# Narrow-head attention on Trainium2: the value products of a step in two bursts of two heads instead of one burst of four

## The chip, the cores and the metric

The kernel runs on one core of one Trainium2 chip. The metric is the device time of one execution in microseconds; the median of several runs is given. The engines are TensorE (matmuls and weight loads), VectorE, ScalarE, GpSimd and the DMA queues, each with an instruction stream of its own, and they meet at semaphores.

## What is computed

The program is a stack of four pre-norm transformer layers on an input of 4 x 1024 tokens with 128 features. Only the attentions of the first two layers are touched. Both have 16 heads of 8 features; layer 0 is causal, layer 1 is not:

```python
scores = jnp.einsum('bthd,bshd->bhts', q, k) / math.sqrt(dk)
scores = jnp.where(causal_mask, jnp.float32(-jnp.inf), scores)   # layer 0
attn = jax.nn.softmax(scores, axis=-1)
out = jnp.einsum('bhts,bshd->bthd', attn, v).reshape(Bx, Tx, D)
...
scores = jnp.einsum('bhqd,bhkd->bhqk', q, k) * SCALE             # layer 1
scores = scores - jnp.max(scores, axis=-1, keepdims=True)
attn = jnp.exp(scores)
attn = attn / jnp.maximum(jnp.sum(attn, axis=-1, keepdims=True), 1e-12)
ctx = jnp.einsum('bhqk,bhkd->bhqd', attn, v)
```

## The kernel before

`narrow_attention` is called for layer 0 (causal) and for layer 1. Its work is cut into 16 units, one for each batch and each group of four heads. A unit needs two things of every query: first the maximum of its scores, then the exponentials and their products with the values.

**The maxima, a unit ahead.** `a_slot` (L1181) multiplies a block of 128 queries with up to 512 keys into one of three banks `slot_ps`, and VectorE reduces it to `part_max` (L1344; L1340 with the mask on the diagonal of layer 0). A unit has 64 such slots in layer 1 and 48 in layer 0. They are worked off four to a step during the steps of the unit before (`shape.ahead`), `lead` = 5 or 6 steps early. Behind the last slot `max_turn` (L1188) transposes the maxima, GpSimd splits them into three bf16 parts, and DMAs put them into `q_op` as extra rows, so that the score product subtracts them.

**The steps.** A step is half the queries (512, `hq`) against one block of 128 keys (`kb`), for all four heads: 16 steps a unit in layer 1; 12 in layer 0, where future blocks are left out and the four blocks on the diagonal of each half stream only 512, 384, 256 and 128 queries. Score products (L1203) are bf16 with 51 rows, two heads `jj` in the two row halves of the array; the pair `e` = 0 or 1 of heads goes to the bank pair `scores[e]`. On the diagonal of layer 0 four small mask products (L1210, 128 columns) follow each pair. ScalarE takes the exponential of a pair (L1321) into `probs`, in one of four buffers, and counts `probs_done`.

**The values.** `values(u, n)` (L1223) multiplies the values of a block with `probs`, in float32, 32 columns of the array for each head, so that the four heads lie in four column groups and write four stripes of one bank `o_ps`. It accumulates over the blocks of a half. At the first block of a half it waits until ScalarE has copied the former half out of the bank (`o_copied`, L1308). Every float32 product is two records in the trace, so a call leaves eight. When a half is done, `o_turn` (L1195) transposes the copy and VectorE divides by the sums.

**The order on TensorE in step n of unit u** is written out by hand. For e = 0: one slot, the score pair 0 (after waiting for the exponential of pair 0 of the step before), one slot. For e = 1 the same. Then the values of step n - 1, all four heads. Then, at three of the steps, a turn. ScalarE's order is: at the second step of a half the copy of the former half, then the two exponentials.

Of the kernel before, what the change touches and what calls it, by code (L numbers as in the profile page):

```python
# [27 lines left out]
UNITS = BATCH * GROUPS  # L28
# [1052 lines left out]
def narrow_attention(nc, name, shape, operands, scale, ctx_nat, consts, floor=None, fills=None, soft=None):  # L1081

    H, S, BANKS = 4, shape.n, 3
    NA = len(shape.slots)
    feats = ctx_nat.shape[1] // TILES
    with ExitStack() as ctx:
# [6 lines left out]
        def sem(n):  # L1093
            return nc.alloc_semaphore(f"{name}_{n}")
# [23 lines left out]
        scores_ready, probs_done, pv_done = sem("scores_ready"), sem("probs_done"), sem("pv_done")  # L1118
# [47 lines left out]
        @block.tensor  # L1166
        def _(te):
            def bank_for(n):
                if n >= BANKS:
                    te.wait_ge(slot_done, n - BANKS + 1)  # L1170
                return slot_ps[n % BANKS]

            def a_slot(u, s):

                j, qt, kh = shape.slots[s]
                g, e, r0 = u % GROUPS, j // 2, (j % 2) * HALF_ROWS
                if s == 0:
                    te.wait_ge(qk_loaded[g], (u // GROUPS + 1) * 16 * N_QK)
                out = bank_for(shape.place["slot", u, s])
                width = shape.slot_width(s)  # L1180
                nc.tensor.matmul(out[:, 0:width], q_op[g][r0:r0 + MAX_ROW, e, qt * P:(qt + 1) * P],  # L1181
                                 k_op[g][r0:r0 + MAX_ROW, e, kh * CH:kh * CH + width], start=True, stop=True).then_inc(slot_ready, 1)

            def max_turn(u):

                te.wait_ge(row_max_done, u + 1)
                out = bank_for(shape.place["max", u, 0])
                nc.tensor.transpose(out[0:H * KB, 0:P], row_max[:], ident[:]).then_inc(slot_ready, 1)  # L1188

            def o_turn(u, hq):  # L1190

                te.wait_ge(o_copied, u * 2 + hq + 1)
                out = bank_for(shape.place["o", u, hq])
                for t in range(CPT):
                    mm = nc.tensor.transpose(out[:, t * P:(t + 1) * P], o_sb[hq][:, t * P:(t + 1) * P], ident[:])  # L1195
                mm.then_inc(slot_ready, 1)

            def score(u, n, e, jj):

                hq, kb = shape.steps[n]  # L1200
                g, off, r0, r1 = u % GROUPS, shape.off(hq, kb), jj * HALF_ROWS, jj * HALF_ROWS + MAX_ROW + 3
                diag = shape.causal and kb >= CPT * hq
                return nc.tensor.matmul(scores[e][:, jj, off:CH], k_op[g][r0:r1, e, kb * P:(kb + 1) * P],  # L1203
                                        q_op[g][r0:r1, e, hq * CH + off:(hq + 1) * CH], start=True, stop=not diag)

            def mask(n, e, jj, h):

                hq, kb = shape.steps[n]
                off, r0 = shape.off(hq, kb), jj * HALF_ROWS
                return nc.tensor.matmul(scores[e][:, jj, off:off + P], ident2[r0:r0 + HALF_ROWS, h, :],  # L1210
                                        mask_b2[r0:r0 + HALF_ROWS, h, :], start=False, stop=h == 1)

            def values(u, n):

                hq, kb = shape.steps[n]
                g, off = u % GROUPS, shape.off(hq, kb)
                te.wait_ge(probs_done, (u * S + n + 1) * 2)
                if n == 0:
                    te.wait_ge(v_spread, u + 1)
                if kb == 0 and u * 2 + hq > 0:  # L1220
                    te.wait_ge(o_copied, u * 2 + hq)
                for j in range(H):
                    mm = nc.tensor.matmul(o_ps[32 * j:32 * (j + 1), off:CH], v_op[g][:, kb, 32 * j:32 * (j + 1)],  # L1223
                                          probs[(u * S + n) % NB][:, j, off:CH], start=kb == 0, stop=n in shape.half_end)
                mm.then_inc(pv_done, 1)

            if shape.causal:
                te.wait_ge(masks_loaded, 48)
            for s in range(NA):
                a_slot(0, s)  # L1230
            max_turn(0)
            for s in shape.head_start():
                a_slot(1, s)
            te.wait_ge(ones_loaded, 16 * 2 * R)
            for u in range(UNITS):
                te.wait_ge(max_loaded[u % GROUPS], (u // GROUPS + 1) * 16 * N_MAX)
                for n in range(S):
                    todo = shape.ahead(u, n)
                    cut = [len(todo) * p // 4 for p in range(5)]
                    gs = u * S + n  # L1240
                    hq, kb = shape.steps[n]
                    diag = shape.causal and kb >= CPT * hq
                    for e in range(2):
                        for v, s in todo[cut[2 * e]:cut[2 * e + 1]]:
                            a_slot(v, s)
                        if gs > 0:
                            te.wait_ge(probs_done, (gs - 1) * 2 + e + 1)
                        score(u, n, e, 1)
                        mm = score(u, n, e, 0)
                        if diag:  # L1250
                            mask(n, e, 1, 0)
                            mask(n, e, 0, 0)
                            mask(n, e, 1, 1)
                            mm = mask(n, e, 0, 1)
                        mm.then_inc(scores_ready, 1)
                        for v, s in todo[cut[2 * e + 1]:cut[2 * e + 2]]:
                            a_slot(v, s)
                    if n > 0:
                        values(u, n - 1)
                    elif u > 0:  # L1260
                        values(u - 1, S - 1)
                    if n == 2 and u > 0:
                        o_turn(u - 1, 1)
                    if n == shape.half_end[0] + 3:
                        o_turn(u, 0)
                    if n == S - shape.lead and u + 1 < UNITS:
                        max_turn(u + 1)
            values(UNITS - 1, S - 1)
            o_turn(UNITS - 1, 1)

        @block.gpsimd
# [688 lines left out]
class CosineShape:  # L1960


    S = 2 * KB
# [1272 lines left out]
```

## Time and profile before

| | |
|---|---|
| median of 3 runs | 3596.66 us (3596.16 to 3596.76) |
| the profiled execution | 3575.11 us, its span 3573.2 us |
| busy in the span | PE 83%, DVE 73%, ACT 60%, POOL 13% |
| attention of layer 0, first to last exponential | about 107.8 to 553 us |
| attention of layer 1, first to last exponential | about 936.8 to 1593.0 us |

The busy share of PE counts the modelled end of each matmul, which overlaps with the next one; differences of start times say more. The shares are means over stages with different limits, so the two attentions have to be read by themselves.

### The profile page before, as it was taken

To read this page: it belongs to the slowest core of one execution; us is meant where nothing else is said; L and a number is where in the kernel's file an instruction comes from. 1 tells how busy PE (TensorE), PEld (TensorE's weight loads), DVE (VectorE), ACT (ScalarE), POOL (GpSimd) and SP (SyncE) were. 2 spreads that over 40 slices of the span, in tenths; PEclk is the share of its full clock that TensorE was granted. 3 is DMA by queue.
4 is the path that set the end of the run, shared out by engine and by line. 5 is a ranking of instruction groups with operands and counts; after the bars stand their busy time and mean duration, and the time that the engine had idled before them with its cause. 6 is when DMAs were issued, how large, how long until landed. Compare 5 with 4: busy or idle time off the path is not lost. (4 is left out here: it accounts for less than half of the span.)

```text
span 3573.2 us, 51682 instructions
## 1 busy us (share of the span) xinstructions
PE 2981.4 (83%) x18320; PEld 1203.9 (34%) x18320; DVE 2616.7 (73%) x6042; ACT 2150.4 (60%) x2740; POOL 451.6 (13%) x633
## 2 busy tenths in 40 slices
PE   5999997896999999985799998967469988889836
PEld 2333333443122222223355555545322222222214
DVE  6999973666999999946566666640868888888821
ACT  2566673323377777773355555522369999899822
POOL 2000001333000000000000000014220011102023
PEclk7899998997799999997899999978779999999968
DMA  4443202343211111000000000011362222221102
GB/s 146 58 106 62 33 13 48 64 80 112 30 27 27 22 22 22 12 3 3 31 1 1 1 7 7 1 54 50 106 140 33 33 33 39 27 30 23 53 24 74
DMA packets 172975, 148.27 MB, mean 41 GB/s; under 512 B 79672, under 2 KB 130632, under 8 KB 172720
## 3 DMA queue, kind: packets, MB, share of 16 engines
q1 hardware_dynamic: 168624, 137.21, 19.2%
q0 software_dynamic: 4096, 7.78, 0.7%
q8 instruction: 145, 2.38, 0.3%
q14 instruction: 110, 0.90, 0.1%
HBM read 95.13 MB, written 49.68 MB: 41 GB/s over the span
## 5 line engine op out<-in xcount | busy, mean ns | idle before, releaser
L1321 ACT ACTIVATE a_probs<-a_scores 128x1024 f32<-128x1024 f32 (+3 forms) x896 | 791.5, 932 | 374.1 <-PE a_scores L1203 233.9
L1344 DVE TENSOR_REDUCE a_part_max<-a_slot_ps 128x1 f32<-128x512 f32 x1280 | 798.6, 684 | 30.9 <-PE a_slot_ps L1181 29.6
L2341 DVE TENSOR_TENSOR a_probs<-a_logit_ps,a_gate 128x1024 f32<-128x1024 f32 x512 | 602.4, 1219 | 98.8 <-ACT a_gate L2200 97.5
L1181 PE MATMUL a_slot_ps<-a_k_op,a_q_op 48*128 48x512 bf16 (+3 forms) x1792 | 579.1, 380 | 95.6 <-DMA a_mask_wide<-in_mask_wide 17.9
L2205 ACT ACTIVATE a_probs<-a_probs 128x2048 f32<-128x2048 f32 x256 | 488.1, 1907 | 7.7 <-DVE a_probs L2341 7.6
L1203 PE MATMUL a_scores<-a_q_op,a_k_op 51*128 51x512 bf16 (+3 forms) x1792 | 452.4, 361 | 7.1 <-ACT a_probs L1321 6.1
L1223 PE MATMUL a_o_ps<-a_probs,a_v_op 128*32 128x512 f32 (+3 forms) x3584 | 437.9, 561 | 1.2 <-ACT a_o_sb L1308 0.6
L1181 PEld LDWEIGHTS a_slot_ps<-a_k_op,a_q_op 48*128 48x128 bf16 x1792 | 150.2, 94 | 697.5 <-DVE a_part_max L1344 469.2
L2106 PE MATMUL a_logit_ps<-space 96*128 96x512 bf16 x1024 | 303.3, 387 | 71.2 <-DVE a_probs L2341 62.4
L2200 ACT ACTIVATE a_gate<-a_diff_ps 128x1024 f32<-128x1024 f32 x256 | 261.6, 1022 | 55.2 <-PE a_diff_ps L2106 47.5
L2119 PE MATMUL a_o_ps<-a_probs,a_v_op 128*32 128x512 f32 x2048 | 274.0, 607 | 7.0 <-DVE a_o_sb L2334 3.1
L1340 DVE CUSTOM_DVE_ANT_0 a_slot_ps<-a_slot_ps,a_mask_wide 128x128 f32<-128x128 f32 (+3 forms) x512 | 237.0, 516 | 5.1 <-PE a_slot_ps L1181 4.1
L757 ACT ACTIVATE a_turned_sb<-a_turn_ps 128x512 f32<-128x512 f32 x192 | 93.6, 488 | 208.0 <-PE a_turn_ps L632 207.8
L747 ACT ACTIVATE space<-space,a_lows 128x128 f32<-128x128 f32 (+7 forms) x256 | 195.2, 767 | 4.0 <-DVE a_lows L841 4.0
L632 PE MATMUL a_turn_ps<-ident_sb,space 128*128 128x128 f32 x1152 | 167.1, 277 | 22.7 <-DVE a_turned_sb L852 18.0
L852 DVE COPY a_turned_sb<-a_turn_ps 128x512 f32<-128x512 f32 x192 | 106.6, 555 | 95.6 <-PE a_turn_ps L632 95.1
L2106 PE MATMUL a_diff_ps<-space 96*128 96x512 bf16 x512 | 157.1, 389 | 15.1 <-DMA a_v_op<-scratch_v 15.1
L841 DVE CUSTOM_DVE_ANT_0 space<-a_score_ps,a_mask 128x512 f32<-128x512 f32 (+3 forms) x256 | 138.7, 587 | 37.3 <-PE a_score_ps L619 37.2
L2106 PEld LDWEIGHTS a_logit_ps<-space 96*128 96x128 bf16 x1024 | 77.0, 98 | 263.9 <-DVE a_probs L2341 219.4
L632 PEld LDWEIGHTS a_turn_ps<-ident_sb,space 128*128 128x128 f32 x1152 | 132.6, 141 | 70.1 <-issue 32.1
L619 PE MATMUL a_score_ps<-a_kT,a_qT 64*128 64x512 f32 (+3 forms) x768 | 152.3, 516 | 1.1 <-DVE a_lows L841 1.0
L646 PE MATMUL a_o_ps<-a_turned_sb,a_v 128*64 128x512 f32 (+3 forms) x768 | 149.9, 512 | 0.0
(400 smaller groups left out, 3758.3 us busy)
## 6 DMA issues: line engine op xcount, KB each, us to landing
e_coef<-coef_dram SPq DMA_DIRECT2D x16, 1024.0 KB, 9.9
a_q_op<-scratch_q SPq DMA_DIRECT2D x384, 32.0 KB
a_k_op<-scratch_k SPq DMA_DIRECT2D x384, 32.0 KB
scratch_q<-p_parts SPq DMA_DIRECT2D x24, 384.0 KB, 3.4
scratch_k<-p_parts SPq DMA_DIRECT2D x24, 384.0 KB, 3.4
space<-scratch_k SPq DMA_DIRECT2D x192, 32.0 KB
space<-scratch_g SPq DMA_DIRECT2D x192, 32.0 KB
space<-scratch_q SPq DMA_DIRECT2D x192, 32.0 KB
```

Of the source, the lines that this page charges most:

```text
L632: mm = nc.tensor.transpose(turn_ps[j][:, t * P:(t + 1) * P], rows_of(u, h, t)[0][:, j, kb * P:(kb + 1) * P], ident[:])
L1181: nc.tensor.matmul(out[:, 0:width], q_op[g][r0:r0 + MAX_ROW, e, qt * P:(qt + 1) * P], k_op[g][r0:r0 + MAX_ROW, e, kh * CH:kh * CH + width] ...
L1203: return nc.tensor.matmul(scores[e][:, jj, off:CH], k_op[g][r0:r1, e, kb * P:(kb + 1) * P], q_op[g][r0:r1, e, hq * CH + off:(hq + 1) * CH] ...
L1223: mm = nc.tensor.matmul(o_ps[32 * j:32 * (j + 1), off:CH], v_op[g][:, kb, 32 * j:32 * (j + 1)], probs[(u * S + n) % NB][:, j, off:CH], sta ...
L1321: nc.scalar.activation(probs[gs % NB][:, 2 * e:2 * e + 2, off:CH], scores[e][:, :, off:CH], ACT.Exp, scale=scale).then_inc(probs_done, 1)
L1340: nc.vector.tensor_tensor_reduce(out=slot[:, 0:w], in0=slot[:, 0:w], in1=mask_wide[:, CH - w:CH], scale=1.0, scalar=-3e38, op0=ALU.add, op ...
L1344: nc.vector.tensor_reduce(part_max[u % 2][:, kh, col:col + 1], slot[:, 0:w], axis=AX.X, op=ALU.max).then_inc(slot_done, 1)
L2106: mm = nc.tensor.matmul(out[:, j, :], ops[g][0][:, j, kb * P:(kb + 1) * P], q[:, j, hq * CH:(hq + 1) * CH], start=True, stop=True)
L2119: mm = nc.tensor.matmul(o_ps[c0:c0 + 32, :], v_op[g][:, kb, j * 32:(j + 1) * 32], probs[gs % 4][:, m, j, :], start=kb == 0, stop=kb == KB - 1)
L2200: nc.scalar.activation(gate[gs % 2][:], diff_ps[:], ACT.Tanh).then_inc(gate_done, 1)
L2205: nc.scalar.activation(tile[:], tile[:], ACT.Exp).then_inc(exp_done, 1)
L2341: nc.vector.tensor_tensor(probs[gs % 4][:, m, :, :], logit_ps[m][:], gate[gs % 2][:], op) \
```

## The change

`values` gets the pair `e` as a third argument. Each call does two of the four heads and waits for the exponential of that pair alone; the call for e = 0 keeps the waits for the spread values and for the copy, the call for e = 1 keeps the count `pv_done`. The calls move into the loop over `e`: the values of pair e of the step before now follow the slots and scores of pair e. At the very end two calls follow one another. `narrow_attention` is used by both layers, so both are changed.

```diff
-            def values(u, n):
+            def values(u, n, e):
 
                 hq, kb = shape.steps[n]
                 g, off = u % GROUPS, shape.off(hq, kb)
-                te.wait_ge(probs_done, (u * S + n + 1) * 2)
-                if n == 0:
+                te.wait_ge(probs_done, (u * S + n) * 2 + e + 1)
+                if n == 0 and e == 0:
                     te.wait_ge(v_spread, u + 1)
-                if kb == 0 and u * 2 + hq > 0:
+                if kb == 0 and e == 0 and u * 2 + hq > 0:
                     te.wait_ge(o_copied, u * 2 + hq)
-                for j in range(H):
+                for j in (2 * e, 2 * e + 1):
                     mm = nc.tensor.matmul(o_ps[32 * j:32 * (j + 1), off:CH], v_op[g][:, kb, 32 * j:32 * (j + 1)],
                                           probs[(u * S + n) % NB][:, j, off:CH], start=kb == 0, stop=n in shape.half_end)
-                mm.then_inc(pv_done, 1)
+                if e == 1:
+                    mm.then_inc(pv_done, 1)
...
                         for v, s in todo[cut[2 * e + 1]:cut[2 * e + 2]]:
                             a_slot(v, s)
-                    if n > 0:
-                        values(u, n - 1)
-                    elif u > 0:
-                        values(u - 1, S - 1)
+                        if n > 0:
+                            values(u, n - 1, e)
+                        elif u > 0:
+                            values(u - 1, S - 1, e)
...
-            values(UNITS - 1, S - 1)
+            for e in range(2):
+                values(UNITS - 1, S - 1, e)
```

## Rows read from the trace of the kernel before

**Rows 1.** Windows, one unit each; columns: length, busy us (instructions) per engine, clock, DMA

```profile
core 0: us, PE busy (x) PEld busy (x) DVE busy (x) ACT busy (x) POOL busy (x), PEclk, DMA share, GB/s
336.39:364.88 28.49, 26.67 (x266) 10.62 (x265) 25.93 (x87) 19.24 (x27) 1.95 (x5) 1.00 0.26 35
...
1188.53:1230.46 41.93, 39.95 (x267) 8.61 (x265) 41.38 (x73) 32.10 (x34) 1.95 (x5) 1.00 0.18 23
...
507.33:531.47 24.14, 22.57 (x242) 8.57 (x243) 13.99 (x48) 19.02 (x26) 1.95 (x5) 1.00 0.01 2
531.47:552.90 21.43, 18.39 (x214) 6.42 (x214) 1.10 (x4) 18.70 (x26) 0.00 (x0) 1.00 0.00 1
1523.97:1561.98 38.01, 36.00 (x243) 7.68 (x240) 28.93 (x52) 31.69 (x34) 1.95 (x5) 1.00 0.01 2
1561.98:1593.01 31.03, 27.41 (x198) 6.22 (x198) 1.44 (x6) 29.91 (x34) 0.00 (x0) 1.00 0.00 1
```

**Rows 2.** Groups of lines, layer 1, 950 to 1550 us; busy, mean ns, idle before

```profile
L1344 DVE TENSOR_REDUCE a_part_max<-a_slot_ps 128x1 f32<-128x512 f32 x918 | 570.1, 683 | 0.8
...
L1181 PEld LDWEIGHTS a_slot_ps<-a_k_op,a_q_op 48*128 48x128 bf16 x917 | 69.4, 93 | 389.9 <-DVE a_part_max L1344 349.5 <-DVE a_nat L1380 23.4 <-issue 14.1
```

**Rows 3.** Timeline of a step of layer 1; start us, length us, instruction

```profile
1199.83 6.25 DVE L1344 TENSOR_REDUCE a_part_max<-a_slot_ps 128x1 f32<-128x512 f32 x10
...
1202.46 0.39 PE L1181 MATMUL a_slot_ps<-a_k_op,a_q_op 48*128 48x512 bf16 x1
...
1202.78 1.07 PE L1223 MATMUL a_o_ps<-a_probs,a_v_op 128*32 128x512 f32 x8
...
1203.78 0.39 PE L1181 MATMUL a_slot_ps<-a_k_op,a_q_op 48*128 48x512 bf16 x1
1203.78 0.60 PE L1203 MATMUL a_scores<-a_q_op,a_k_op 51*128 51x512 bf16 x2
...
1204.01 0.64 PE L1181 MATMUL a_slot_ps<-a_k_op,a_q_op 48*128 48x512 bf16 x2
...
1204.42 1.94 ACT L1321 ACTIVATE a_probs<-a_scores 128x1024 f32<-128x1024 f32 x2 [0.55 <-PE a_scores L1203]
```

**Rows 4.** Timeline of TensorE, layer 0: shorter bursts, each with the next start

```profile
341.46 0.85 PE L1223 MATMUL a_o_ps<-a_probs,a_v_op 128*32 128x384 f32 x8
342.25 0.66 PE L1195 MATMUL a_slot_ps<-ident_sb,a_o_sb 128*128 128x128 f32 x4
...
344.39 0.64 PE L1223 MATMUL a_o_ps<-a_probs,a_v_op 128*32 128x256 f32 x8
344.96 0.39 PE L1181 MATMUL a_slot_ps<-a_k_op,a_q_op 48*128 48x512 bf16 x1
...
346.39 0.43 PE L1223 MATMUL a_o_ps<-a_probs,a_v_op 128*32 128x128 f32 x8
...
346.75 0.39 PE L1181 MATMUL a_slot_ps<-a_k_op,a_q_op 48*128 48x512 bf16 x1
```

**Rows 5.** Timeline of TensorE in other stages: float32 products of 512 columns

```profile
623.68 1.02 PE L2564 MATMUL e_g_ps<-e_xnT,e_g_w 128*128 128x512 f32 x2
624.53 1.02 PE L2567 MATMUL e_u_ps<-e_xnT,e_u_w 128*128 128x512 f32 x2
...
1760.29 1.94 PE L646 MATMUL a_o_ps<-a_turned_sb,a_v 128*64 128x512 f32 x8
1762.16 1.12 PE L666 MATMUL a_spare_ps<-a_xnT,a_w_q 128*128 128x512 f32 x2
```

**Rows 6.** Timeline of layer 1: copies out of the values' bank, a turn

```profile
1021.65 1.06 PE L1223 MATMUL a_o_ps<-a_probs,a_v_op 128*32 128x512 f32 x8
...
1022.78 0.60 ACT L1308 ACTIVATE a_o_sb<-a_o_ps 128x512 f32<-128x512 f32 x1
...
1219.66 0.28 PE L1188 MATMUL a_slot_ps<-ident_sb,a_row_max 128*32 128x128 f32 x1
...
1579.78 0.60 ACT L1308 ACTIVATE a_o_sb<-a_o_ps 128x512 f32<-128x512 f32 x1
...
1580.53 1.06 PE L1223 MATMUL a_o_ps<-a_probs,a_v_op 128*32 128x512 f32 x8 [0.19 <-ACT a_o_sb L1308]
```

## The prediction

> **What bounds the kernel now.** I read the views in this order: the windows by unit, the groups of lines, the timeline of one step, then the timeline of other stages with similar matmuls.
>
> The windows show both attentions as a row of equal units: 28.49 us each in layer 0 and 41.93 us in layer 1, at full granted clock, with the last two units of each layer shorter [rows 1]. VectorE is busy 25.93 of 28.49 us and 41.38 of 41.93 us. Its maxima are reduced one slot after another: 918 reductions of 683 ns with 0.8 us idle in all, while the weight loads of the next slots wait 349.5 us for them [rows 2]. So in layer 1 VectorE sets the pace; ten reductions fill 6.25 us, hence 0.625 us a slot and 2.49 us for a step of four slots [rows 3]. That TensorE reads as 39.95 us busy is a trap: the view counts ends of matmuls that overlap. What TensorE can do is read from starts.
>
> **TensorE's own time for a step, layer 1** [rows 3]. A slot product (48 rows) and a score product (51 rows) sit in different row halves and start together at 1203.78; the next pair starts at 1204.01, so a pair costs 0.225 us (0.23 in the rounded row). From a slot's start to the values burst are 0.32 us (1202.46 to 1202.78), 0.09 more than a pair. The burst of four heads (eight records, as each float32 product is two passes) runs from 1202.78 to the next start at 1203.78: 1.00 us. A step is four slots and four scores, so four pairs: 4 x 0.225 + 0.09 + 1.00 = 1.99 us. TensorE thus has 0.50 us of slack in 2.49.
>
> **What the change does.** It removes nothing: 3584 value records stay, so do their weight loads, and no transfer is moved. It splits each burst in two, each of two heads, one behind each score pair. The disputed cost is one burst of two heads. The four heads of a burst go to four column groups of the array and stream at once, each in two passes. The trace has no such two-head burst of 32 columns; its bounds are these:
> - lower, if time goes with heads: half of 1.00, 0.50 us;
> - upper, if time goes with the streamed columns: the same 1.00 us.
>
> Two rows lie near. A float32 product over all 128 columns (two records, 512 streamed) takes 0.85 us (623.68 to 624.53), 0.43 a pass: no cheaper and no dearer than four heads side by side. In layer 2 a block is exactly two heads in two column groups (of 64); two blocks of 512 run from 1760.29 to 1762.16, 1.87 us, four passes of 0.43 and 0.15 us around them [rows 5]. Time goes with passes, not heads. I take 2 x 0.43 + 0.13 = 0.99 us for two heads.
>
> The page "TensorE: Matmul & The Clock Gate" of the Trainium skill, Part 3 (packing small matmuls), gives a packed group as one matmul plus about 4 ns for each further tile. By it two heads are 16 ns cheaper than four over both passes, 14 us over 896 bursts, and the total would be about 3839 instead of 3845. The row of layer 2 is closer to no difference than to half.
>
> Each burst has a change of array shape on both sides (64-row tiles to 32-column tiles and back): 0.09 us ahead, about 0.14 behind the two passes, both inside the figures above. They are paid twice a step now.
>
> **New step, layer 1.** 4 x 0.225 + 2 x 0.09 + 2 x 0.99 = 3.06 us, above VectorE's 2.49 and ScalarE's 2 x 0.97 [rows 3]. TensorE becomes the bound, the waits for maxima vanish, and 0.57 us a step is added. The added wait on the exponentials costs nothing: the score pair ahead of each burst has already waited for the same count.
>
> **The copies.** A value product that starts a new half waits until ScalarE has copied the last one out of its bank. Now it comes half a step earlier: formerly two score pairs stood between, now one. A copy starts 1.13 us after the start of the burst it waits for (1021.65 to 1022.78), and the gated burst starts 0.75 us after a copy's start (1579.78 to 1580.53) [rows 6]: 1.88 us. TensorE is there after 0.99 + 0.225 + 0.32 = 1.54. It stalls 0.34, twice a unit; queued behind it are the score pair and slots, so everybody waits. In layer 0 both gated bursts follow a burst of 128 columns (0.36 us), and the copy is queued on ScalarE behind the second exponential of the step. From the start of the second half that exponential ends after some 0.64 + 0.97 us [rows 3] plus 0.3 for masks or the first exponential, 1.9; with 0.75 this is 2.65, against TensorE there after some 1.5. Stall 1.1, twice a unit (an estimate; from 0 to 1.3).
>
> **Layer 1.** A unit: 16 x 3.06 = 49.0, turns 1.4 (two of 0.66 and one of 0.28 us [rows 4, 6], less 0.07 each that overlaps with what follows), stalls 0.7: 51.1 against 41.93, +9.2. Fourteen such units: +129. The fifteenth has no slots in its last 5 steps, each 2 x 0.225 cheaper: 48.9 against 38.01, +10.9. The last has none: 16 x 2.61 + 1.2 + 0.7, less half a step to its last exponential, 42.4 against 31.03: +11.4, and 1.0 for the second burst of the very end. Layer 1: +152.
>
> **Layer 0.** A unit has 12 steps. By the code its bursts are six of 512 columns, two each of 384, 256 and 128: 1.00, 0.79, 0.57 and 0.36 [rows 3, 4], in sum 9.4 us. Slots, scores and masks stream 22528 columns when paired, 44 times 512: 44 x 0.225 = 9.9 us. With 12 x 0.09 and 1.4 of turns TensorE needs 21.8 of the 28.49, so 6.7 us are slack. It is spread unevenly, but even the longest steps of maxima (four slots, 2.5 us) stay under the new 3.0 of a full step. New: 9.9 + 24 x 0.09 + 18.6 + 1.4 = 32.1, stalls 2.2: 34.3, so +5.8. Fourteen: +81. The fifteenth (24 slots fewer, 2.0 us): 32.3 against 24.14, +8.2. The last: 34.3 less 4.1 for slots and 1 for its last half step, 29.2 against 21.43: +7.8. Layer 0: +97.
>
> **Sum.** +249 us: on the profiled execution (3575.11, span 3573.2) 3824; the median of the runs is 21.5 us above that execution, so 3596.66 + 249 = 3845.7, say 3845. All else in the program is before or after these units by its data and stays.
>
> **The rivals.**
> *Two heads cost half (other side: not slower).* If a pass took half its time with two column groups, the two bursts would be 2 x 0.43 + 2 x 0.13 = 1.12 in place of 0.99, the step 0.90 + 0.18 + 1.12 = 2.20, under VectorE's 2.49. Layer 1 would not move; in layer 0 VectorE could at best close its 2.56 idle us a unit, since slots no longer sit behind a 1.00 us burst: 16 x 2.56 = 41, so 3556 at best and 3597 at least. It decides once a two-head burst is under some 0.70 us. Against it: the 1.87 us of layer 2 [rows 5]. Chance 0.06, split between faster and no change.
> *The shape changes cost more when they come twice.* The skill's page "TensorEngine Tiling (Array Packing)", key properties, says that changing the tiling mode drains the engine; the trace agrees in that 0.09 and 0.14 us surround a burst. It would speak against the change even if streaming were free. As a mechanism in rows: if weight loads can no longer be fetched ahead and each new crossing costs the whole wait of 0.2 us more, 448 steps add 90 us: 3935. Nothing in the rows asks for it, as bursts of 0.36 us pay the same edges [rows 4]. Chance 0.09.
> *The stalls at the copies are absorbed.* Then layer 0 is 35 and layer 1 is 11 us less: 3800. This is the low end of my case, not a case apart.
>
> **How the numbers follow.** My case has chance 0.85: time 3845, range 3800 (no stalls) to 3885 (stalls at 1.3, VectorE starving TensorE 0.5 us a unit in the short steps of layer 0, and the edges 0.03 dearer: 6 + 8 + 27). That range leaves 0.15 for the rivals and a little of the case itself, so it holds 0.8. A measurement of this kernel tells 0.2% (7 us) from no change. Faster 0.035, within 0.2% 0.025, slower 0.94.
>
> **What would show it.** After: two-head bursts of 0.99 us from start to next start; unit periods of about 51 and 34 us in place of 41.93 and 28.49; VectorE with idle time before its reductions, released by slot products; no slot load waiting for a maximum in layer 1; a wait for the copy at L1308 before two bursts a unit. Layers 2 and 3 unchanged. I am wrong if the burst takes 0.5 to 0.7 us, or if VectorE still has no gaps in layer 1.

## The result and the profile after

The changed kernel takes 3843.97 us (median of 4 runs, 3838.0 to 3846.81) against 3596.41 us before: a ratio of 1.0688, 95% interval 1.0675 to 1.0701. It is 247.6 us slower; forecast were 249 us and 3845.

The windows of one unit of each layer, and of the last two of each, in the changed kernel (columns as in [rows 1]):

```profile
core 0: us, PE busy (x) PEld busy (x) DVE busy (x) ACT busy (x) POOL busy (x), PEclk, DMA share, GB/s
383.13:417.60 34.47, 32.98 (x267) 11.58 (x269) 26.84 (x87) 20.11 (x26) 1.96 (x5) 1.00 0.21 29
1244.16:1294.90 50.74, 50.24 (x267) 9.31 (x269) 42.77 (x73) 33.76 (x34) 1.96 (x5) 1.00 0.14 19
589.93:621.96 32.03, 30.62 (x241) 9.95 (x243) 14.15 (x48) 20.11 (x26) 1.96 (x5) 1.00 0.01 2
621.96:651.41 29.45, 27.19 (x210) 8.01 (x213) 1.10 (x4) 19.63 (x26) 0.00 (x0) 1.00 0.00 1
1751.56:1799.92 48.36, 47.86 (x245) 9.06 (x247) 29.86 (x52) 33.77 (x35) 1.96 (x5) 1.00 0.01 1
1799.92:1842.60 42.68, 41.75 (x198) 8.31 (x200) 1.44 (x6) 32.65 (x33) 0.00 (x0) 1.00 0.00 1
```

The same work and the same number of instructions take 50.74 us in place of 41.93 in layer 1 and 34.47 in place of 28.49 in layer 0 [rows 1], at full clock in all of them. Fourteen units and the last two give 14 x 8.81 + 10.35 + 11.65 = 145.3 us for layer 1 and 14 x 5.98 + 7.9 + 8.0 = 99.6 us for layer 0: 245 us of the 247.6 lost.

The timeline of a half step of layer 1 shows where it goes (to be set beside [rows 3]):

```profile
1148.45 0.39 PE L1181 MATMUL a_slot_ps<-a_k_op,a_q_op 48*128 48x512 bf16 x1
1148.45 0.60 PE L1203 MATMUL a_scores<-a_q_op,a_k_op 51*128 51x512 bf16 x2
...
1148.68 0.38 PE L1181 MATMUL a_slot_ps<-a_k_op,a_q_op 48*128 48x512 bf16 x1
1148.87 1.29 DVE L1346 TENSOR_REDUCE a_part_max<-a_slot_ps 128x1 f32<-128x512 f32 x2 [0.23 <-PE a_slot_ps L1181]
...
1148.99 1.05 PE L1223 MATMUL a_o_ps<-a_probs,a_v_op 128*32 128x512 f32 x4
...
1149.97 0.39 PE L1181 MATMUL a_slot_ps<-a_k_op,a_q_op 48*128 48x512 bf16 x1
```

Four value records (two heads) hold TensorE from 1148.99 to 1149.97, 0.98 us; eight records held it 1.00 us [rows 3]. The half step is 1.52 us, the step 3.04, and there is no gap between TensorE's instructions. The reductions, which had 0.8 us of idle time in 600 us of layer 1 [rows 2], now wait for slot products; so says their group in 1060 to 1780 us, and so do the waits of that stretch:

```profile
L1346 DVE TENSOR_REDUCE a_part_max<-a_slot_ps 128x1 f32<-128x512 f32 x909 | 582.9, 686 | 98.7 <-PE a_slot_ps L1181 98.1
```

```profile
DVE a_part_max L1346 <- PE a_slot_ps L1181: 98.1, 385, 0.6
...
PE a_o_ps L1223 <- ACT a_o_sb L1310: 7.0, 28, 0.2
```

The second wait is the new stall at the copy. Its place in layer 0 shows a burst of 128 columns, the slots and scores behind it, the copy behind the exponentials, and the gated burst. The last two lines are the next half step, with four mask products in it and no stall:

```profile
384.07 0.41 PE L1223 MATMUL a_o_ps<-a_probs,a_v_op 128*32 128x128 f32 x4
...
384.41 0.33 PE L1181 MATMUL a_slot_ps<-a_k_op,a_q_op 48*128 48x384 bf16 x1
...
385.09 0.59 ACT L1310 ACTIVATE a_o_sb<-a_o_ps 128x512 f32<-128x512 f32 x1
...
385.83 1.05 PE L1223 MATMUL a_o_ps<-a_probs,a_v_op 128*32 128x512 f32 x4 [0.80 <-ACT a_o_sb L1310]
...
386.81 0.39 PE L1181 MATMUL a_slot_ps<-a_k_op,a_q_op 48*128 48x512 bf16 x1
...
387.41 1.05 PE L1223 MATMUL a_o_ps<-a_probs,a_v_op 128*32 128x512 f32 x4
```

The two profiled spans differ by 271.8 us, 27 more than the attentions. The surplus lies outside the units, 22 us of it behind layer 1, where both kernels run the same instructions. The profiled execution of before was 21 us under the median of its runs and that of after 3 us over its own, and the granted clock behind layer 1 reads 0.91 in the one and 0.90 in the other. So this part is taken for a difference between two executions and not of the kernels; the medians leave only 3 us outside the attentions.

### The profile page after: what moved, and what is told of

Read it like the earlier page. It is cut to its first block and busy times, and to the rows that moved or that the text cites. A ratio compares the mean times of both kernels' runs of the same rounds, so it can differ in the third digit from the quotient of the medians.

```text
span 3845.0 us, 51682 instructions
## 1 busy us (share of the span) xinstructions
PE 3277.9 (85%) x18320; PEld 1245.6 (32%) x18320; DVE 2651.3 (69%) x6042; ACT 2194.1 (57%) x2740; POOL 452.5 (12%) x633
## 5 line engine op out<-in xcount | busy, mean ns | idle before, releaser
L1323 ACT ACTIVATE a_probs<-a_scores 128x1024 f32<-128x1024 f32 (+3 forms) x896 | 834.1, 933 | 578.0 <-PE a_scores L1203 383.0
L1346 DVE TENSOR_REDUCE a_part_max<-a_slot_ps 128x1 f32<-128x512 f32 x1280 | 817.7, 685 | 149.5 <-PE a_slot_ps L1181 147.3
L1223 PE MATMUL a_o_ps<-a_probs,a_v_op 128*32 128x512 f32 (+3 forms) x3584 | 861.8, 560 | 29.5 <-ACT a_o_sb L1310 29.4
L1181 PE MATMUL a_slot_ps<-a_k_op,a_q_op 48*128 48x512 bf16 (+3 forms) x1792 | 568.7, 378 | 41.4 <-DMA a_mask_wide<-in_mask_wide 16.0
L1203 PE MATMUL a_scores<-a_q_op,a_k_op 51*128 51x512 bf16 (+3 forms) x1792 | 485.5, 361 | 0.1
L1181 PEld LDWEIGHTS a_slot_ps<-a_k_op,a_q_op 48*128 48x128 bf16 x1792 | 130.5, 94 | 689.3 <-DVE a_part_max L1346 465.8
L1223 PEld LDWEIGHTS a_o_ps<-a_probs,a_v_op 128*32 128x32 f32 x3584 | 130.7, 108 | 303.6 <-ACT a_probs L1323 224.4
L1291 POOL TENSOR_TENSOR a_max_parts<-a_neg_max,a_zeros 32x128 bf16<-32x128 f32 x32 | 12.5, 390 | 1269.6 <-DVE a_neg_max L1361 1269.6
```

What stands on the lines that cost most here:

```text
L1323: nc.scalar.activation(probs[gs % NB][:, 2 * e:2 * e + 2, off:CH], scores[e][:, :, off:CH], ACT.Exp, scale=scale).then_inc(probs_done, 1)
L1346: nc.vector.tensor_reduce(part_max[u % 2][:, kh, col:col + 1], slot[:, 0:w], axis=AX.X, op=ALU.max).then_inc(slot_done, 1)
```

## Experiments

The kernel before was timed again beside each group of experiments, at 3584.26 us beside the first group and 3594.75 beside the second, so it is the ratios that are compared and not the times. Theory: a burst costs its passes over the streamed columns, whatever the number of heads side by side, so the split doubles that cost.

**Split calls, side by side.** Both calls of two heads stay, with their own waits, but stand together at the end of the step.

```diff
+                    for e in range(2):
                         if n > 0:
                             values(u, n - 1, e)
```

> The calls stay split (two heads each, each with its own wait), but both stand behind the second score pair, one right behind the other. Pass theory (a value product costs its streamed passes, and heads side by side share them): the four column groups are adjacent again and stream together, a burst of 1.00 us, VectorE sets the pace of layer 1, units of 41.93 and 28.49 us, 3597 us. Rival (a call of two heads costs a burst of its own wherever it stands): two bursts of 0.99 less one pair of edges, a step of 2.8 us in layer 1, at least 3680 us.

Measured: 3582.61 us against 3584.26, ratio 0.9992 (0.9982 to 1.0001). A window of one unit's length in layer 1, and one burst with the next start:

```profile
1188.53:1230.46 41.93, 39.94 (x267) 8.61 (x265) 41.36 (x73) 32.09 (x34) 1.95 (x5) 1.00 0.15 23
```

```profile
1203.00 1.06 PE L1223 MATMUL a_o_ps<-a_probs,a_v_op 128*32 128x512 f32 x8
1204.00 0.39 PE L1181 MATMUL a_slot_ps<-a_k_op,a_q_op 48*128 48x512 bf16 x1
```

The window reads as before [rows 1], and the eight records take 1.00 us. Two calls next to each other stream as one burst of four; what costs is that slots and scores stand between them.

**Four heads, half the columns.** As many bursts and shape changes as in the changed kernel, but each burst does all heads on half of the queries. The product that opens a sum stays whole.

```diff
-                te.wait_ge(probs_done, (u * S + n) * 2 + e + 1)
+                if kb == 0 and e == 0:
+                    return
+                te.wait_ge(probs_done, (u * S + n + 1) * 2)
...
-                for j in (2 * e, 2 * e + 1):
-                    mm = nc.tensor.matmul(o_ps[32 * j:32 * (j + 1), off:CH], v_op[g][:, kb, 32 * j:32 * (j + 1)],
-                                          probs[(u * S + n) % NB][:, j, off:CH], start=kb == 0, stop=n in shape.half_end)
+                mid = (off + CH) // 2
+                c0, c1 = (off, CH) if kb == 0 else ((off, mid), (mid, CH))[e]
+                for j in range(H):
+                    mm = nc.tensor.matmul(o_ps[32 * j:32 * (j + 1), c0:c1], v_op[g][:, kb, 32 * j:32 * (j + 1)],
+                                          probs[(u * S + n) % NB][:, j, c0:c1], start=kb == 0,
+                                          stop=n in shape.half_end and e == 1)
```

> Two bursts a step as in the changed kernel, behind the same score pairs, but each does all four heads on half of the query columns (the first product of a half, which opens the sum, stays whole at the end of its step). As many changes of the array's shape, half the columns in each pass. Pass theory: bursts of 0.57 us, a step of 0.90 + 0.18 + 1.14 = 2.22 us on TensorE, under VectorE's 2.49; layer 1 stays at 41.93 a unit, layer 0 at 28.49 or up to 2 us less, 3565 to 3600 us. Rival (the cost lies in the shape changes, paid twice as often): 14 of 16 steps slower as in the changed kernel, about 3810 us.

Measured: 3554.81 us against 3584.26, ratio 0.9914 (0.9897 to 0.9930): faster than both kernels. Timeline of a burst and the next start and of ten reductions, then the windows of one unit of each layer:

```profile
1163.25 0.64 PE L1227 MATMUL a_o_ps<-a_probs,a_v_op 128*32 128x256 f32 x8
...
1163.82 0.39 PE L1181 MATMUL a_slot_ps<-a_k_op,a_q_op 48*128 48x512 bf16 x1
...
1165.45 6.06 DVE L1351 TENSOR_REDUCE a_part_max<-a_slot_ps 128x1 f32<-128x512 f32 x10
```

```profile
354.50:382.05 27.55, 27.00 (x346) 11.76 (x345) 25.88 (x87) 19.88 (x26) 1.96 (x5) 1.00 0.26 36
1170.00:1210.42 40.42, 39.97 (x379) 11.70 (x377) 40.24 (x73) 33.32 (x35) 1.95 (x5) 1.00 0.18 25
```

A burst is 0.57 us. Shape changes twice a step are not what costs: they are all here, and the kernel is faster. It also corrects a reading of mine. The unit takes 40.42 us, 1.5 us less than in [rows 1] for the same reductions, and ten reductions fill 6.06 us in place of 6.25 [rows 3]. So VectorE was not quite the bound before. By the starts in the two traces, nearly all reductions now start 0.60 us after the last. In the kernel before three of four do (0.60 to 0.61), and the one whose slot stands behind the burst starts after 0.68. A burst of 1.00 us thus delayed one slot a step by some 0.08 us, and two of 0.57 no longer do.

**One head and three heads.** The changed kernel with another cut: `for j in ((0,), (1, 2, 3))[e]`.

> The changed kernel with the heads cut one and three in place of two and two. Pass theory: the burst of one head takes as long as that of three, 0.98 and 0.99 us, and the time is that of the changed kernel, 3844 us within 8. Rival (a burst has a part that grows with its heads): the burst of one head is clearly shorter than that of three, by 0.1 us or more.

Measured: 3830.63 us against 3584.26, ratio 1.0685 (1.0667 to 1.0703), that of the changed kernel. The timeline of TensorE, layer 1:

```profile
1151.67 1.04 PE L1223 MATMUL a_o_ps<-a_probs,a_v_op 128*32 128x512 f32 x2
1152.64 0.39 PE L1181 MATMUL a_slot_ps<-a_k_op,a_q_op 48*128 48x512 bf16 x1
...
1153.18 1.06 PE L1223 MATMUL a_o_ps<-a_probs,a_v_op 128*32 128x512 f32 x6
1154.17 0.39 PE L1181 MATMUL a_slot_ps<-a_k_op,a_q_op 48*128 48x512 bf16 x1
```

One head (x2) holds TensorE 0.97 us, three heads (x6) 0.99. With two heads at 0.98 and four at 1.00 a head adds 0.01 us to a burst, where a burst of its own costs 0.97.

**One pass.** The changed kernel with `probs` and `v_op` in bf16; the value products are less precise, everything else is the same.

```diff
-        self.v = [sb(f"v_op{i}", [P, KB, self.vcols]) for i in range(GROUPS)]
+        self.v = [sb(f"v_op{i}", [P, KB, self.vcols], BF16) for i in range(GROUPS)]
...
-        probs = [sb(f"probs{i}", [P, H, CH]) for i in range(NB)]
+        probs = [sb(f"probs{i}", [P, H, CH], BF16) for i in range(NB)]
```

> The changed kernel with exponentials and values in bf16, so that a value product is one pass at one column a clock in place of two passes at half that rate; precision of these products is lower, the order and the number of bursts and shape changes are those of the changed kernel. Pass theory: a burst of two heads takes 0.22 + 0.13 = 0.35 us, a step of layer 1 takes TensorE 0.90 + 0.18 + 0.70 = 1.78 us, VectorE's 2.39 us set the pace, 0.98 to 1.00 of before. Rival (the second burst costs by being there, with its shape changes and its place): the ratio stays over 1.03.

Measured: 3613.94 us against 3594.75, ratio 1.0047 (1.0030 to 1.0064). Neither expectation holds as it stands. The timeline of TensorE has the burst of 0.33 us that was expected, and the windows of two units of layer 1 tell what else happened (the last column but two is the granted clock):

```profile
1053.94 0.39 PE L1223 MATMUL a_o_ps<-a_probs,a_v_op 128*32 128x512 bf16 x2
1054.27 0.39 PE L1181 MATMUL a_slot_ps<-a_k_op,a_q_op 48*128 48x512 bf16 x1
```

```profile
1042.27:1082.34 40.07, 39.29 (x202) 10.60 (x201) 39.90 (x73) 33.28 (x34) 1.95 (x5) 1.00 0.16 24
1211.10:1262.30 51.20, 50.84 (x203) 9.33 (x201) 42.95 (x73) 33.72 (x35) 1.95 (x5) 0.50 0.14 19
```

At 2.4 GHz a unit takes 40.07 us, VectorE's pace, as the theory has it. In other units the granted clock is 0.50, that is 1.2 GHz, and the same unit takes 51.20. In layer 0 the clock moved too: one unit took 27.02 us at 1.00, another 31.20 at 0.72. The rival is out, since at full clock the second bursts are there and cost nothing; the gain is lost to the clock.

**Four heads behind the first pair.** The kernel before, its one burst moved half a step forward.

```diff
-                    if n > 0:
-                        values(u, n - 1)
-                    elif u > 0:
-                        values(u - 1, S - 1)
+                        if e == 0 and n > 0:
+                            values(u, n - 1)
+                        elif e == 0 and u > 0:
+                            values(u - 1, S - 1)
```

> One burst of four heads as before, but behind the first score pair of the step in place of the second. Pass theory: nothing doubled; the copy out of the bank is met half a step earlier, as in the changed kernel, but the stall of 0.3 us (layer 1) and 0.7 to 0.8 us (layer 0), twice a unit, is covered by TensorE's slack of 0.5 us a step: 3597 us within 10. Rival (the early place of the products behind the copy is a main part of the loss): 32 units with 0.6 to 1.6 us more, 3615 to 3640 us.

Measured: 3731.75 us against 3584.26, ratio 1.0380 (1.0315 to 1.0446). Both expectations missed. Windows of two units of layer 0 and one of layer 1, then the timeline of layer 1:

```profile
217.78:248.41 30.63, 25.91 (x266) 10.68 (x265) 25.92 (x87) 19.56 (x27) 1.96 (x6) 1.00 0.42 104
316.14:350.30 34.16, 29.67 (x267) 11.33 (x265) 26.07 (x87) 19.55 (x26) 1.96 (x6) 0.85 0.20 29
1099.59:1145.53 45.94, 40.55 (x266) 9.68 (x265) 41.17 (x73) 32.33 (x35) 1.96 (x6) 1.00 0.14 21
```

```profile
1350.92 0.60 PE L1203 MATMUL a_scores<-a_q_op,a_k_op 51*128 51x512 bf16 x2
1350.98 1.94 ACT L1321 ACTIVATE a_probs<-a_scores 128x1024 f32<-128x1024 f32 x2 [0.89 <-PE a_scores L1203]
...
1352.06 1.06 PE L1223 MATMUL a_o_ps<-a_probs,a_v_op 128*32 128x512 f32 x8 [0.16 <-ACT a_probs L1321]
...
1354.78 1.06 PE L1223 MATMUL a_o_ps<-a_probs,a_v_op 128*32 128x512 f32 x8 [0.16 <-ACT a_probs L1321]
```

The bursts are 2.72 us apart and each waits for an exponential. A burst needs both exponentials of the step before; the second one's scores stood behind the last burst. The loop is burst (1.00), scores to exponential (0.64), exponential (1.02), semaphore (0.06): 2.72. Sixteen times the 0.23 us over 2.49 are 3.7 of the 4.0 us that a unit of layer 1 has become longer.

The loop is not the whole loss. In layer 0 the granted clock fell to 0.85 from about 270 us on, and a unit took 34.16 us in place of 30.63. By the trace nine units were longer by 2.9 to 3.5 us each, some 30 us of the profiled execution. The four runs spread with the clock: 3691.78 us at a mean of 0.922, the others 3727.92 to 3742.25 at 0.903 to 0.909.

**The same, a step older.** The burst behind the first pair takes the step before last (`values(u - (n < 2), (n - 2) % S)`, and two calls at the end).

> One burst of four heads behind the first score pair, as in early4, but of the step before last, so that its exponentials are a step older. Loop theory (early4 was slow because the burst waits for the second exponential of the step just before, whose scores stood behind the burst of that step: 0.64 + 1.02 + 0.06 + 1.00 = 2.72 us around the loop): the loop is gone, steps of layer 1 fall from 2.72 to between 2.39 and 2.50, 0.99 to 1.01 of before. Rival (a burst of 1.00 us behind the first pair starves VectorE of slots, wherever its operands come from): the steps stay at 2.7, ratio about 1.04.

Measured: 3609.78 us against 3594.75, ratio 1.0043 (1.0030 to 1.0056). Two second score pairs that follow one another on the timeline of layer 1, then windows of one unit of each layer, a copy and the score pair behind it:

```profile
1300.09 0.60 PE L1203 MATMUL a_scores<-a_q_op,a_k_op 51*128 51x512 bf16 x2
...
1302.58 0.60 PE L1203 MATMUL a_scores<-a_q_op,a_k_op 51*128 51x512 bf16 x2
```

```profile
264.78:292.36 27.58, 25.91 (x266) 10.27 (x265) 25.82 (x87) 19.51 (x27) 1.95 (x6) 1.00 0.45 109
1096.54:1139.85 43.31, 40.18 (x266) 8.72 (x265) 41.38 (x73) 32.32 (x35) 1.95 (x5) 1.00 0.16 23
```

```profile
1153.53 0.60 ACT L1307 ACTIVATE a_o_sb<-a_o_ps 128x512 f32<-128x512 f32 x1 [0.96 <-PE a_o_ps L1223]
...
1155.10 0.39 PE L1203 MATMUL a_scores<-a_q_op,a_k_op 51*128 51x512 bf16 x2 [0.83 <-ACT a_probs L1320]
```

The step is 2.49 us again and the ratio within the 0.99 to 1.01 of the loop theory, so the loop is confirmed and the rival is out. The unit of layer 1 is still 43.31 us and not 41.93, while that of layer 0 is 27.58, under the 28.49 of before. The product that ends a half now comes a step later, but the copy kept its place in ScalarE's order. ScalarE waits 0.96 us for it, the exponentials behind the copy are late, and TensorE's scores wait 0.83, twice a unit.

The split of the studied change is free of the loop, as each burst of two waits only for the exponential of its own pair: none of TensorE's waits in 1060 to 1780 us is for an exponential.

**First products whole.** The changed kernel; only the products that wait for a copy stay unsplit at the end of their step.

```diff
-                        if n > 0:
-                            values(u, n - 1, e)
-                        elif u > 0:
-                            values(u - 1, S - 1, e)
+                        if gs > 0 and shape.steps[(n - 1) % S][1] != 0:
+                            values(u - (n == 0), (n - 1) % S, e)
+                    if gs > 0 and shape.steps[(n - 1) % S][1] == 0:
+                        for e in range(2):
+                            values(u - (n == 0), (n - 1) % S, e)
```

> The changed kernel, but the products of the first key block of a half (the ones that wait for the copy) keep all four heads in one burst at the end of their step; two steps a unit are unsplit, all others split. Copy theory: each of these steps loses one burst and its edge (1.08 us, of which VectorE's 2.39 us a step lets 0.7 through) and the whole stall (0.32 us in layer 1, about 0.75 in layer 0): 2.0 us a unit in layer 1, 2.9 in layer 0, 78 us in all, a ratio of 1.047 to before. Rival (the waits for the copy cost nothing of their own): 2 x 0.7 us in all 32 units, 45 us, a ratio of 1.056.

Measured: 3770.86 us against 3594.75, ratio 1.0485 (1.0468 to 1.0503). The rival's 1.056 is outside. Windows of one unit of each layer, then two bursts of the changed kernel between which the copy is waited for:

```profile
254.87:286.75 31.88, 31.58 (x266) 11.31 (x265) 26.64 (x87) 19.89 (x27) 1.96 (x6) 1.00 0.34 101
1240.00:1288.99 48.99, 48.73 (x267) 9.33 (x265) 42.60 (x73) 33.53 (x35) 1.95 (x5) 1.00 0.11 20
```

```profile
1245.58 1.05 PE L1223 MATMUL a_o_ps<-a_probs,a_v_op 128*32 128x512 f32 x4
...
1247.42 1.05 PE L1223 MATMUL a_o_ps<-a_probs,a_v_op 128*32 128x512 f32 x4 [0.25 <-ACT a_o_sb L1310]
```

A unit of layer 1 has got back 1.75 us of the 2.0 expected, one of layer 0 2.59 of 2.9. In layer 1 the two parts can be read apart. From one burst to the next are 1.84 us where the copy is waited for and 1.52 elsewhere, a stall of 0.32. The unsplit step takes 2.47 us, 0.57 less than two half steps. Twice both is 1.78. The stall at the copy is a real part of the loss.

**Layer 0 alone.** The split calls are interleaved only where `shape.causal` holds, and stand together in layer 1.

> The change in layer 0 alone; in layer 1 both calls of a step stand together at its end. If the two layers pay independently, as the sum had it: layer 0's 99 us and nothing of layer 1, a ratio of 1.027 to before, units of 34.47 us and 41.93 us. Rival (one layer's slower end changes what the next does): another ratio by more than 0.003.

Measured: 3695.35 us against 3594.75, ratio 1.0283 (1.0266 to 1.0300), 101 us where the units of layer 0 had given 99.6. The layers pay independently.

## Why the prediction was right

**The disputed cost.** Two heads were put at 0.99 us between 0.50 and 1.00; they take 0.98. The choice by the nearest rows [rows 5] carried the forecast, and one against three heads and the half-column bursts show the reason: passes over columns are paid, not heads. The 16 ns that the packing rule of "TensorE: Matmul & The Clock Gate", Part 3, in the Trainium skill would take off for two heads fewer is about what is seen, 1.00 to 0.98.

**The bound moves to TensorE.** Predicted steps of 3.06 us are 3.04; units 51.1 against 50.74 and 34.3 against 34.47; the shortened units 48.9, 42.4, 32.3 and 29.2 against 48.36, 42.68, 32.03 and 29.45. Layer 1 cost 145 us (152 forecast), layer 0 100 (97).

**A sign that did not come.** No slot load of layer 1 was to wait for a maximum any more. The changed kernel still shows such waits, 333.7 us in a stretch of 720, where the kernel before had 349.5 in 600 [rows 2]:

```profile
PEld a_slot_ps L1181 <- DVE a_part_max L1346: 333.7, 398, 0.8
```

Each is about 0.84 us and stands behind a burst: it is the time in which the burst of values streams, put down to the maximum that was the last thing waited for. The same 0.84 us stands once a step in the 349.5, so that wait did not show that VectorE sets the pace. What showed it was the row of reductions without gaps; gaps between them did come as forecast (98.1 us).

**The stalls at the copy.** In layer 1 the stall was put at 0.34 us; by the starts of bursts it is 0.32, and TensorE's idle time, which counts from the modelled end of a matmul, is 7.0 / 28 = 0.25. In layer 0 1.1 was too much. In the window shown 1.42 us lie between slot and gated burst (384.41 to 385.83), where the same columns need 0.54 by the prediction's own prices (1024 paired columns, 2 x 0.225 + 0.09): a stall of 0.88, and 0.89 at the other gated burst of the unit. Together these are 1.8 us a unit where 2.2 was forecast. What made up for it is some 0.6 us of TensorE's own time. It does not lie in how masks pair: from 386.81 to the burst at 387.41, masks and all, are 0.60 us, which is what 1152 paired columns at 0.225 us for 512 and 0.09 give. About 0.3 us of it stand in the one step with both turns, 0.1 in a step of 128 columns; the rest is spread. Two errors of opposite sign, so layer 0's 3 us of agreement is partly luck.

By these numbers (an estimate from one unit of each layer) the stalls are 16 x 0.6 + 16 x 1.8 = 38 us of the loss, and the doubled bursts with their edges nearly all the rest.

**VectorE as the bound of before.** Right to 4%: with shorter bursts the same unit takes 40.42 us, not 41.93. The idle time of 0.8 us in [rows 2] hid this, since reductions overlap by their recorded ends (683 ns long, 0.60 us from start to start), and a delay shorter than the overlap does not count as idle.

**The rivals.** "Two heads cost half" is refuted by the 0.97 us of a single head, "the shape changes cost more when they come twice" by the half-column bursts, with as many changes in 14 of 16 steps and a faster kernel.

**The sum against the median** held although the two profiled executions stand differently to their medians (21 us under, 3 over); had the forecast been compared with the span of after, it would have been 23 us short (3573.2 + 249 against 3845.0) through no fault of its terms.

## What to carry to other kernels

Column groups of the array share a pass over the streamed operand. Cutting such a burst by heads pays the pass again (0.97 us for one head, 1.00 for four); cutting it by streamed columns pays only the edges and left this kernel 0.9% faster than before, because the engine fed between bursts was starved less. Before a product is moved, follow its operand around the loop: an exponential one step old cost 0.23 us a step that a two steps old one did not. Then follow what waits for the product: moved back a step, it made the copy late, and with it the exponentials behind the copy.

## What the runs showed of the hardware unasked

Two calls of two heads, with separate waits, stream together as one burst of four when nothing stands between them (ratio 0.9992). With the value products in bf16 TensorE was granted 1.2 GHz in some units of layer 1 and 2.4 GHz in others, in one kernel and with the same instructions; before the fall its units read 39.29 us busy of 40.07. The other kernels kept 1.00 in the units of layer 1 that were read. With the burst of four moved forward the clock fell in layer 0, though its value products are those of the kernel before: its first units there read 25.91 us busy of 30.63 at 1.00, the later ones a mean of 0.85, where the kernel before kept 1.00 with 26.67 of 28.49. Which units fall was not settled.
